# A graph layer on one core: register loads a group ahead, feed-forward weights in quarters, rounded rows in two buffers and earlier in their engine's order, a last mean in six matmuls, and multiplies in the router's wait

## The chip, the core and the metric

The program runs on one core of a Trainium2 chip. The metric is the time of one execution on the device, in microseconds (us), as the median of several runs.

## What is computed

`x` has 6250 rows of 256 values. The reference, cut to what matters (`_layernorm`, `mix` and `ffn` stand for longer functions, told in words below):

```python
xn = _layernorm(x)
m  = xn[src] @ weights[:d] + edge_attr_256 @ weights[d:]      # 106250 edges, dst sorted
h  = segment_sum(m * norm[dst][:, None], dst, 6250)           # norm = rsqrt(degree)
x  = x + (h + h_bias) + mix(xn)                               # linear attention, 8 heads, GELU block
y  = _layernorm(x)
logits = mean(y) @ Wr + br      # one router decision for all rows: two of eight experts
x  = x + layernorm(y + sum_e w_e * (gelu(y @ W1[e] + b1[e]) @ W2[e] + b2[e]))
```

The router needs the mean over all rows, so no feed-forward work on weights can start before the last row of the first part is there. All of it is float32.

## The kernel before

**Engines and semaphores.** Each engine (PE = TensorE, DVE = VectorE, ACT = ScalarE, POOL = GpSimd, SP = SyncE) has a program of its own, written by hand in the order in which it runs. It takes its instructions in that order, and `wait_ge(semaphore, value)` holds back everything behind it on that engine.

**Edge phase.** The 106250 edges are cut in 70 groups (`NG`) of three steps (`TS`), with the loop variables `t` and `q = 3 * t + i`. A step fills one of six slots of `ring`: the edges' own rows by SP (`edge_load`), and four gathers of the source rows by POOL (L562). Both wait for `s_seg` of the step that used the slot before. PE sums each strip of 128 edges into 32 destinations (`strip_sums`, L926), and turns the sums of a group over (`transposes`, L935 and L938). DVE adds them to `acc` (`sums`, L1367 and L1372): for each of four strips it first loads a place in `acc` from SBUF into a register (`value_load`, L1367), then adds there (L1372). Every two to three groups 250 rows are complete (`DONE`). PE then turns their degrees (`turn_degrees`, L948, which waits for `s_acc`, the count of DVE's additions) and multiplies by the weights (`project`, L957). The attention and mix steps are spread between these steps on all engines.

**Router.** After the last group come `last_rows`, the last rows' part of the mean (`mean_last`, L1072, eight one-column multiplies), the router's chain of small operations on one partition (DVE L1593 to L1633 and three exponentials on ACT, L872 to L877), and the loads of the chosen experts' weights by SP. ACT first normalizes the last 250 rows (`norm_last`, L734) and then loads its table of exponentials. PE turns these rows (`turn_last`, L1062), waits for the router's weights, spreads them (L1205), and starts on the feed-forward part when both halves of the first weights are split.

**Feed-forward phase.** It runs over 25 chunks `c` of 250 rows, through `chunks`: `step(0)`, `step(1)`, a loop over `step(2)` to `step(21)`, and `step(22)` to `step(24)`. All float32 operands are split into a rounded value (`_hi`, an ACT copy) and a rest (`_lo`, a DVE subtraction), and each product is three multiplies. Per chunk:

- SP loads the turned rows into `xtl`, two buffers (`fetch_turned`, L502), and stores the result (`store`, L527);
- ACT copies `xtl` to `xf_hi` (`rows_hi`), DVE makes `xf_lo` (`rows_lo`, L1638);
- PE multiplies by the first weights (`first`, L1179, 48 multiplies in four banks `q`), ACT applies the GELU (L847) and rounds to `h_hi`, DVE makes `h_lo` (L1643): both are called `hidden`;
- PE multiplies by the second weights (`second`, L1190, 48 multiplies);
- DVE adds the rows and takes mean and variance (`added`, L1651 on), POOL makes scale and offset (L618, L620), ACT applies them (`normed`, L857), DVE applies gamma and beta (`finish`, L1668 and L1671), and `store` sends the rows out.

On PE `step(c)` is `first(c + 1)`, `second(c)`. On ACT it is `rows(c + 2)`, `hidden(c + 1)`, `rows_hi(c + 2)`, `normed(c - 1)`. On DVE it is `hidden(c + 1)`, `rows_lo(c + 2)`, `finish(c - 1)`, `added(c)`. SP runs this loop, the same before and after the change but for the last chunk's store:

```python
fetch_turned(2)
for c in range(NC):
    if c + 3 < NC:
        fetch_turned(c + 3)
    store(c)                 # waits for finish(c)
```

So the load of chunk `c + 4` is issued only when the store of chunk `c` has been.

Of the kernel before, what the change touches and what calls it, by code (L numbers as in the profile page):

```python
# [83 lines left out]
def gps_layer(nc, x, src_l, dst_l, edges, wgnn, hbias, wkv_l, wq_t, bkv_l, bq_l, kln_g, kln_b, vln_g, vln_b,  # L84
              w1, b1_l, w2, b2, wr, br, fw1, fb1_l, fw2, fb2, gamma, beta, out):
    ctx = ExitStack()
    with ctx:
# [120 lines left out]
        xf_hi = sbx("xf_hi", [P, KC, CW], F32R)  # L208
        xf_lo = sbx("xf_lo", [P, KC, CW], F32R)
# [41 lines left out]
        s_w2, s_rw, s_fb = s_wkv, s_src, s_par  # L251
        W2, ROUTER, FFN_ROWS = 16 * 2 + 16, 16 + 32, 16 * 11 + 16 * 6
# [153 lines left out]
        def _(sp):  # L406
# [114 lines left out]
            sp.dma_start(grow[:, :], gamma.partition_broadcast(TN)).then_inc(s_fb, 16)  # L521
            sp.dma_start(berow[:, :], beta.partition_broadcast(TN)).then_inc(s_fb, 16)
# [11 lines left out]
            sp.wait_ge(s_out[0], 16 * (NC - NC // 2))  # L534
# [4 lines left out]
        def _(pool):  # L539
# [62 lines left out]
            pool.wait_ge(s_fb, FFN_ROWS)  # L602
# [7 lines left out]
            def step(c, u, i):  # L610
                if not (isinstance(c, int) and c + 1 >= NC):
# [3 lines left out]
                                   ALU.add).then_inc(s_xb[u], 1)  # L615
                pool.wait_ge(s_vx, c * 2 + 2)
# [10 lines left out]
        def _(act):  # L627
# [197 lines left out]
            norm_last()  # L825
# [55 lines left out]
            rows_hi(0, 0, 0)  # L881
            act.wait_ge(s_ra, 3)
# [8 lines left out]
            act.wait_ge(s_fb, FFN_ROWS)  # L891
# [860 lines left out]
```

## Time and profile before

| | |
|---|---|
| median of 3 runs | 1591.93 us (1590.64 to 1594.72) |
| profiled execution, its own time | 1609.85 us |
| its span, first to last instruction | 1608.1 us |
| PE busy | 1082.5 us, 67% of the span |
| POOL, DVE, ACT busy | 919.3, 685.6 and 530.8 us |
| mean granted TensorE clock | 0.85 |
| edge phase, about | 100 to 1287 us |
| feed-forward phase, about | 1309 to 1608 us |

The durations below come from the profiled execution, which took 17.9 us more than the median run. A busy share is an average over phases; the stages are read from windows of the trace. "Idle before, released by" names the instruction whose semaphore ended a wait, "remote" one that the trace couldn't name, and "issue" time in which the engine's own sequencer was at work or at something that the profile doesn't show: register loads stand there.

### The profile page before, as it was taken

What the parts mean: (1) busy time and instruction counts of PE and PEld (TensorE: products, weight loads), DVE (VectorE), ACT (ScalarE), POOL (GpSimd) and SP (SyncE); (2) the same over time, 40 slices, a digit from 0 to 9 for tenths busy, and PEclk for the clock granted to TensorE, in tenths of its full rate; (3) what the DMA queues carried; (4) which work ended last, traced back from release to release, by engine and by line L of the source; (5) the groups of instructions that cost most, each with busy time, mean ns of one, the idle gap of its engine ahead of it and who ended that gap; (6) DMA issues with size and microseconds to landing.
All of it is one profiled execution on the core that took longest, in us unless ns stands there. A gap on an engine that the chain in (4) does not pass through costs nothing.

```text
span 1608.1 us, 20064 instructions
## 1 busy us (share of the span) xinstructions
PE 1082.5 (67%) x6075; PEld 687.8 (43%) x6075; DVE 685.6 (43%) x1732; ACT 530.8 (33%) x1116; POOL 919.3 (57%) x974
## 2 busy tenths in 40 slices
PE   0155767666566666755776666666577759999997
PEld 0012323323223322323432333333343459999997
DVE  4733434334333344322233233242322446677675
ACT  3611111111111111111213333243233257767673
POOL 6166666676666666666666666666666103434342
PEclk9977888888877888877889778787888869999999
DMA  9975555565555555476777768777767230111111
GB/s 252 303 222 177 176 174 167 180 196 183 182 172 179 179 182 183 131 242 203 215 226 221 223 214 244 229 216 229 245 211 219 85 99 27 51 44 45 49 40 40
DMA packets 189376, 275.67 MB, mean 171 GB/s; under 512 B 19840, under 2 KB 160296, under 8 KB 188037
## 3 DMA queue, kind: packets, MB, share of 16 engines
q1 hardware_dynamic: 139424, 152.85, 31.7%
q0 software_dynamic: 39888, 108.97, 22.5%
q10 hardware_dynamic: 9975, 12.80, 2.3%
q8 instruction: 38, 0.62, 0.2%
q14 instruction: 51, 0.42, 0.1%
HBM read 248.95 MB, written 25.60 MB: 171 GB/s over the span
## 4 chain that ended last, share of the span: by engine, by line
PE 33%; another core or an unknown queue 23%; issue 18%; DVE 13%; ACT 6%; DVEq 5%; DMA 2%; SPq 1%; ACTq 0%; POOL 0%; POOLq 0%
PE bank L1190 8%; PE bank L1179 4%; PE ps_t L1179 4%; DVEq L1367 4%; PE bank L926 4%; PE bank L957 4%; PE bank L1009 3%; DVE acc L1372 2%; PE bank L1040 2%; DVE lnst L1403 1%; PE bank L1052 1%; PE ps_t L938 1%; DVE xc L1399 1%; DVE st L1227 1%
## 5 line engine op out<-in xcount | busy, mean ns | idle before, releaser
L562 POOL DMA_INDIRECT ring<-xn_table,src_sb x807 | 785.0, 973 | 441.0 <-issue 224.9
L926 PE MATMUL bank<-ring,s 128*32 128x512 f32 x1662 | 272.2, 667 | 79.6 <-DVE s L1332 38.7
L1009 PE MATMUL bank<-wstage,xt 128*125 128x512 f32 x200 | 124.2, 748 | 108.3 <-ACT xt L629 73.1
L1372 DVE TENSOR_TENSOR acc<-acc,ps_t 128x160 f32 x277 | 89.2, 322 | 203.1 <-issue 155.2
L629 ACT ACTIVATE xt<-bank 128x250 f32<-128x250 f32 (+1 forms) x75 | 33.5, 447 | 307.7 <-remote 262.4
L1040 PE MATMUL bank<-xt,p_sb 128*128 128x250 f32 x200 | 73.6, 533 | 85.6 <-ACT xt L629 44.3
L957 PE MATMUL bank<-wg,acc 128*125 128x256 f32 x400 | 123.7, 471 | 7.6 <-issue 7.6
L926 PEld LDWEIGHTS bank<-ring,s 128*32 128x32 f32 x1662 | 42.3, 115 | 197.4 <-issue 147.4
L1643 DVE TENSOR_TENSOR h_lo<-h,h_hi 128x512 fp32r<-128x512 f32 x100 | 95.8, 967 | 49.0 <-ACT h_hi L629 49.0
L618 POOL TENSOR_TENSOR rx<-vex,half 125x2 f32<-125x2 f32 x25 | 17.5, 701 | 171.8 <-DVE nmx L1664 171.8
L1190 PE MATMUL bank<-fw_hi,h_hi 128*125 128x256 f32 x400 | 111.7, 279 | 0.0
L1190 PE MATMUL bank<-fw_hi,h_lo 128*125 128x256 f32 x400 | 111.7, 279 | 0.0
L1190 PE MATMUL bank<-fw_lo,h_hi 128*125 128x256 f32 x400 | 111.6, 279 | 0.0
L1341 DVE TENSOR_TENSOR pair<-s 128x128 f32<-128x128 f32 x70 | 20.4, 291 | 202.5 <-remote 178.2
L1009 PEld LDWEIGHTS bank<-wstage,xt 128*125 128x125 f32 x200 | 41.0, 228 | 150.1 <-ACT xt L629 78.1
L957 PEld LDWEIGHTS bank<-wg,acc 128*125 128x125 f32 x400 | 92.6, 238 | 28.1 <-issue 10.2
L1040 PEld LDWEIGHTS bank<-xt,p_sb 128*128 128x128 f32 x200 | 52.6, 276 | 101.9 <-ACT xt L629 48.2
L1399 DVE TENSOR_TENSOR xc<-bank,bkv 125x512 f32<-125x512 f32 x50 | 34.4, 687 | 119.6 <-remote 105.9
L629 ACT ACTIVATE fl<-bank 128x512 f32<-128x512 f32 x70 | 41.4, 592 | 128.5 <-remote 108.3
L703 ACT ACTIVATE kvn<-xc 125x512 f32<-125x512 f32 x50 | 31.4, 628 | 153.2 <-DVE xc L1399 99.7
L1190 PEld LDWEIGHTS bank<-fw_hi,h_hi 128*125 128x125 f32 x400 | 74.3, 186 | 0.0
L1190 PEld LDWEIGHTS bank<-fw_lo,h_hi 128*125 128x125 f32 x400 | 74.2, 185 | 0.0
(224 smaller groups left out, 2147.5 us busy)
## 6 DMA issues: line engine op xcount, KB each, us to landing
ring<-edges SPq DMA_DIRECT2D x207, 512.0 KB
ring<-xn_table,src_sb POOLq DMA_INDIRECT x807
xnr<-xn_table SPq DMA_DIRECT2D x25, 250.0 KB
xch<-x SPq DMA_DIRECT2D x25, 250.0 KB
base_rows<-xch ACTq DMA_DIRECT2D x25, 250.0 KB
xt_cols<-xte ACTq DMA_DIRECT2D x25, 250.0 KB
xtl<-xt_cols SPq DMA_DIRECT2D x25, 250.0 KB, 4.9
out<-res SPq DMA_DIRECT2D x25, 250.0 KB
```

Of the source, the lines that this page charges most:

```text
L562: pool.indirect_dma_start(out=to, out_offset=None, in_=rows, in_offset=bass.IndirectOffsetOnAxis(ap=index, axis=0),).then_inc(done, 16)
L629: return nc.scalar.activation(o, i, ACT.Copy)
L926: mm = pe.matmul(ps_seg[t % 2][j * W:(j + 1) * W, :], lhsT=s32[:, t % 3, j * TS + i, :], rhs=ring[:, u, j, :], start=i == 0, stop=i == TS ...
L957: mm = pe.matmul(to, lhsT=acc[:, o, a:a + TN], rhs=wg[:, o, :], start=o == 0, stop=o == 2 * KC - 1)
L1009: mm = pe.matmul(ps_kv[0:TN, :], lhsT=xt[:, n % 2, c, 0:TN], rhs=wstage[:, c, :], start=c == 0, stop=c == KC - 1)
L1040: mm = pe.matmul(ps_kv[:, f * CW:f * CW + CN], lhsT=p_sb[:, o, f * P:(f + 1) * P], rhs=xt[:, (NT + c) % 2, o, :], start=o == 0, stop=o == ...
L1179: mm = pe.matmul(bank[q][:, (f % 2) * CW:(f % 2 + 1) * CW], lhsT=a, rhs=b, start=n == 0, stop=n == len(ops) - 1)
L1190: mm = pe.matmul(ps_o[u][0:TN, j * D:(j + 1) * D], lhsT=a, rhs=b, start=n == 0, stop=n == len(ops) - 1)
L1367: bases = [v.value_load(brow[0:1, t * ST + j:t * ST + j + 1], min_val=0, max_val=RN) for j in strips(t)]
L1372: v.tensor_tensor(acc[:, :, ds(b, W)], acc[:, :, ds(b, W)], planes[:, :, j * W:(j + 1) * W], ALU.add).then_inc(s_acc, 1)
L1399: v.tensor_tensor(xc[:, :], ps_kv[0:TN, :], bkv[:, :], ALU.add).then_inc(s_xc, 1)
L1643: v.tensor_tensor(h_lo[:, u, 2 * q:2 * q + 2, :], h32[:, 2 * q:2 * q + 2, :], h_hi[:, u, 2 * q:2 * q + 2, :].bitcast(F32), ALU.subtract).t ...
```

## The change

1. `sums` gets its registers from `strip_bases`, which is called for the next group right after this group's additions.
2. `xf_hi` and `xf_lo` get two buffers. `rows_hi(c + 2)` and `rows_lo(c + 2)` now stand ahead of `hidden(c + 1)` in ACT's and DVE's step.
3. The first weights are rounded and split in quarters; `first(0)` waits for a quarter at a time, and PE's waits for the second weights and for `b2w` stand ahead of `second(0)` and `second(1)`.
4. Gamma and beta have a semaphore of their own (`s_gb`); ACT's first `hidden` waits for the biases alone.
5. The last part of the mean is four one-column and two two-column multiplies. `norm_last` and `keep_last` move into the gaps between the exponentials.
6. PE runs 18 extra multiplies (`spin`) before it waits for the router's weights and 14 after; nothing reads their results.
7. The last chunk's second product, sums, scaling and store run in two halves.

```diff
@@ sync
             def store(c):
                 rows = out[c * CN:(c + 1) * CN, :].rearrange("(t p) d -> p t d", p=TN)
-                sp.wait_ge(s_res[c % 2], c // 2 + 1)
-                sp.dma_start(rows, res[:, c % 2, :, :]).then_inc(s_out[c % 2], 16)
+                if c < LAST:
+                    sp.wait_ge(s_res[c % 2], c // 2 + 1)
+                    sp.dma_start(rows, res[:, c % 2, :, :]).then_inc(s_out[c % 2], 16)
+                else:
+                    for j in range(2):
+                        sp.wait_ge(s_res[c % 2], c // 2 + 1 + j)
+                        sp.dma_start(rows[:, j, :], res[:, c % 2, j, :]).then_inc(s_out[c % 2], 16)
@@ scalar
-            norm_last()
             nc.scalar.activation(rt[0:1, 15, 0:1], ones[0:1, 0:1], ACT.Exp)
...
             def rows_hi(c, u, i):
                 act.wait_ge(s_tl[u], i * 16 + 16)
-                wait_past(act, s_g1, c * (FC // 2))
-                copy(xf_hi[:, :, 0:CN], xtl[:, u, :, :]).then_inc(s_xfh, 1)
+                wait_past(act, s_g1, (c - 1) * (FC // 2))
+                copy(xf_hi[:, u, :, 0:CN], xtl[:, u, :, :]).then_inc(s_xfh, 1)
...
                 if not (fixed and c + 2 >= NC):
                     rows(c + 2, u, i + 1)
+                if not (fixed and c + 2 >= NC):
+                    rows_hi(c + 2, u, i + 1)
                 if not (fixed and c + 1 >= NC):
                     hidden(c + 1, 1 - u, i + u)
-                if not (fixed and c + 2 >= NC):
-                    rows_hi(c + 2, u, i + 1)
...
             nc.scalar.activation(rt[0:1, 2, :], rt[0:1, 1, :], ACT.Exp, bias=rs[0:1, 1:2]).then_inc(s_ra, 1)
-            keep_last()
+            norm_last()
             act.wait_ge(s_rd, 16)
             nc.scalar.activation(rt[0:1, 9, :], rt[0:1, 8, :], ACT.Exp, bias=rs[0:1, 5:6]).then_inc(s_ra, 1)
+            keep_last()
...
             for j in range(2):
                 act.wait_ge(s_fw1[j], FW)
-                copy(fw1_hi[:, :, j * F:(j + 1) * F], fw1_st[:, j, :, :]).then_inc(s_w1h, 1)
+                for a in range(0, F, F // 2):
+                    copy(fw1_hi[:, :, j * F + a:j * F + a + F // 2], fw1_st[:, j, :, a:a + F // 2]).then_inc(s_w1h, 1)
...
-            act.wait_ge(s_fb, FFN_ROWS)
+            act.wait_ge(s_fb, BIASES)
@@ tensor
-                for h in range(KC):
-                    ops = [op for t in range(2 * LAST, NT) for op in ((x2[:, t, h * P:(h + 1) * P], r2[:, t:t + 1]), (ones[0:TN, :], nmr2[:, t:t + 1]))]
-                    for n, (a, b) in enumerate(ops):
-                        mm = pe.matmul(ps_f[:, h:h + 1], lhsT=a, rhs=b, start=n == 0, stop=n == len(ops) - 1)
+                for t in range(2 * LAST, NT):
+                    for h in range(KC):
+                        pe.matmul(ps_f[:, h:h + 1], lhsT=x2[:, t, h * P:(h + 1) * P], rhs=r2[:, t:t + 1], start=t == 2 * LAST, stop=False,
+                                  skip_group_check=True)
+                for t in range(2 * LAST, NT):
+                    mm = pe.matmul(ps_f[:, 0:KC], lhsT=ones[0:TN, :], rhs=nmr2[:, t:t + 1].broadcast_to([TN, KC]), start=False, stop=t == NT - 1,
+                                   skip_group_check=True)
...
-                    if f % 2 == 0 and not (isinstance(c, int) and c == 0):
+                    if f % 2 == 0 and isinstance(c, int) and c == 0:
+                        pe.wait_ge(s_w1l, 2 + q + 1)
+                    elif f % 2 == 0:
                         pe.wait_ge(s_gel, c * FC + (2 * q + 2 - FC))
...
+            def spin(n):
+
+                for t in range(n):
+                    pe.matmul(bank[0][0:TN, 0:D], lhsT=ident[0:TN, 0:TN], rhs=x2[:, t, :], start=True, stop=True)
+
+            spin(18)
             pe.wait_ge(s_top, 2)
             pe.matmul(ps_y[:, 0:2], lhsT=ones[0:1, :], rhs=rt[0:1, 13, 0:2], start=True, stop=True).then_inc(s_bp, 1)
-            pe.wait_ge(s_w1l, 4)
+            spin(14)
             first(0, 0, 0)
@@ vector
-            def sums(t):
-
-                bases = [v.value_load(brow[0:1, t * ST + j:t * ST + j + 1], min_val=0, max_val=RN) for j in strips(t)]
+            def strip_bases(t):
+
+                return [v.value_load(brow[0:1, t * ST + j:t * ST + j + 1], min_val=0, max_val=RN) for j in strips(t)]
+
+            def sums(t, bases):
+
                 v.wait_ge(s_tp, t + 1)
...
                 if i == 2 and 1 <= t <= NG:
-                    sums(t - 1)
+                    sums(t - 1, bases)
+                    bases = strip_bases(t) if t < NG else None
...
+            def added_last(j):
+
+                u, i = LAST % 2, LAST // 2
...
+                v.wait_ge(s_g2[u], i + 1 + j)
+                v.tensor_tensor(o_sb[:, u, j, :], ([ps_kv, ps_acc][u], bank[0])[j][0:TN, 0:D], xlb[:, u, j, :], ALU.add).then_inc(s_od[u], 1)
...
+            def finish_last():
...
             def step(c, u, i):
                 fixed = isinstance(c, int)
+                if not (fixed and c + 2 >= NC):
+                    rows_lo(c + 2, u, i + 1)
                 if not (fixed and c + 1 >= NC):
                     hidden(c + 1, 1 - u, i + u)
-                if not (fixed and c + 2 >= NC):
-                    rows_lo(c + 2, u, i + 1)
+                if fixed and c == LAST:
+                    added_last(0)
                 if not (fixed and c == 0):
                     finish(c - 1, 1 - u, i + (u - 1))
-                added(c, u, i)
...
+                if fixed and c == LAST:
+                    added_last(1)
+                else:
+                    added(c, u, i)
```

ACT's instructions of `step(22)`, the last that rounds a chunk's turned rows, before the change (`h32` is written by the GELUs, `h_hi` by `hidden`'s copies, `res` by `normed`):

```order
L833 ACTIVATE xl<-x2,nmr2,r2 125x256 x2
L847 ACTIVATE h32<-bank0,fb1c 128x256 x2
L629 ACTIVATE h_hi<-h32 128x512
L847 ACTIVATE h32<-bank1,fb1c 128x256 x2
L629 ACTIVATE h_hi<-h32 128x512
L847 ACTIVATE h32<-ps_t,fb1c 128x256 x2
L629 ACTIVATE h_hi<-h32 128x512
L847 ACTIVATE h32<-ps_t,fb1c 128x256 x2
L629 ACTIVATE h_hi<-h32 128x512
L629 ACTIVATE xf_hi<-xtl 128x2x250
L857 ACTIVATE res<-o_sb,bnx,rx 125x256 x2
```

And of the same step with the change:

```order
L845 ACTIVATE xl<-x2,nmr2,r2 125x256 x2
L642 ACTIVATE xf_hi<-xtl 128x2x250
L859 ACTIVATE h32<-bank0,fb1c 128x256 x2
L642 ACTIVATE h_hi<-h32 128x512
L859 ACTIVATE h32<-bank1,fb1c 128x256 x2
L642 ACTIVATE h_hi<-h32 128x512
```

In these rows the copy of the turned rows (`xf_hi`) has moved from behind four GELU pairs to ahead of them; `normed` (`res`) stays last. The loop's steps 2 to 21 have the same order.

PE between the last part of the mean and the first product, before:

```order
L1072 MATMUL bank4<-r2,x2 128x1
L1072 MATMUL bank4<-nmr2,ones 128x1
L1200 MATMUL ps_t<-wr_sb,mean_c 1x8 x2
L1062 MATMUL bank5<-ident,xle 128x125 x4
L1205 MATMUL ps_t<-rt,ones 128x2
```

And with the change:

```order
L1086 MATMUL bank4<-r2,x2 128x1 x4
L1089 MATMUL bank4<-nmr2,ones 128x2 x2
L1227 MATMUL ps_t<-wr_sb,mean_c 1x8 x2
L1077 MATMUL bank5<-ident,xle 128x125 x4
L1234 MATMUL bank0<-x2,ident 125x256 x18
L1238 MATMUL ps_t<-rt,ones 128x2
L1234 MATMUL bank0<-x2,ident 125x256 x14
L1199 MATMUL bank0<-xf_hi,fw1_hi 128x256
```

The spreading of the router's weights (L1205, now L1238) stands behind 18 new multiplies, and the first product behind 14 more.

## Rows read from the trace of the kernel before

**Rows 1.** Windows: us, busy PE, PEld, DVE, ACT, POOL, granted clock, DMA share, GB/s.

```profile
120.00:1270.00 1150.00, 748.95 (x3464) 377.10 (x3464) 405.65 (x1068) 267.64 (x572) 752.75 (x774) 0.82 0.65 199
1290.40:1314.30 23.90, 10.94 (x52) 10.37 (x53) 10.21 (x36) 13.46 (x23) 0.00 (x0) 0.50 0.47 156
1321.10:1324.50 3.40, 3.40 (x19) 3.40 (x18) 0.11 (x1) 2.44 (x5) 3.23 (x3) 0.50 0.26 73
1333.45:1580.73 247.28, 247.28 (x2114) 247.28 (x2114) 173.05 (x308) 176.64 (x372) 95.61 (x88) 1.00 0.16 44
```

**Rows 2.** Waits in 120 to 1270 us: total us, times, longest.

```profile
DVE acc L1372 <- issue: 148.8, 60, 5.3
POOL ring L562 <- remote: 144.5, 61, 4.0
PE ps_t L948 <- DVE acc L1372: 48.3, 14, 8.2
DVE acc L1372 <- ACT acc L629: 18.9, 8, 2.5
```

**Rows 3.** Timeline of DVE at one group: start, us, idle before in brackets.

```profile
637.15 0.69 DVE L1399 TENSOR_TENSOR xc<-bank,bkv 125x512 f32<-125x512 f32 x1 [2.00 <-remote]
639.84 1.69 DVE L1372 TENSOR_TENSOR acc<-acc,ps_t 128x160 f32 x4 [2.00 <-issue]
```

**Rows 4.** Timeline of all engines at the edge phase's end.

```profile
1271.09 0.30 PE L935 MATMUL ps_t<-counts,ones_r 128*128 128x128 f32 x1 [1.91 <-DVE acc L1372]
...
1275.54 1.69 DVE L1372 TENSOR_TENSOR acc<-acc,ps_t 128x160 f32 x4 [2.53 <-issue]
...
1277.37 0.37 PE L935 MATMUL ps_t<-counts,ones_r 128*128 128x32 f32 x1 [3.08 <-DVE acc L1372]
```

**Rows 5.** Timeline of all engines: a hot product, and the router's start.

```profile
1283.71 3.72 PE L957 MATMUL bank<-wg,acc 128*125 128x256 f32 x16
...
1290.85 0.56 PE L1072 MATMUL bank<-r,x 125*128 125x1 f32 x2 [2.99 <-issue]
...
1294.60 1.28 ACT L826 ACT_TABLE_LOAD   x1
...
1296.00 0.28 ACT L872 ACTIVATE rt<-rt,rs 1x8 f32<-1x8 f32 x1
```

**Rows 6.** Timeline of all engines at the start of the feed-forward phase.

```profile
1301.00 0.58 PE L1205 MATMUL ps_t<-rt,ones 1*128 1x2 f32 x2 [5.02 <-DVEq L1633]
...
1308.76 0.58 PE L1179 MATMUL bank<-xf_hi,fw_hi 128*128 128x256 f32 x1 [7.17 <-DVE fw_lo L1690]
...
1320.43 0.36 PE L1179 MATMUL bank<-xf_hi,fw_hi 128*128 128x256 f32 x1 [2.23 <-DVE b2w L1706]
```

**Rows 7.** The chain that ended last, at one feed-forward step.

```profile
1333.45 2.83 PE bank L1179 x24
...
1339.10 5.59 PE bank L1190 x48
```

**Rows 8.** Timeline of ACT over one feed-forward step.

```profile
1340.55 0.61 ACT L629 ACTIVATE xf_hi<-xtl 128x500 fp32r<-128x500 f32 x1
1341.06 1.08 ACT L857 ACTIVATE res<-o_sb,bnx,rx 125x256 f32<-125x256 f32 x2
...
1346.23 0.84 ACT L847 ACTIVATE h<-bank,fb1c 128x256 f32<-128x256 f32 x2 [3.10 <-PE bank L1179]
...
1351.85 0.61 ACT L629 ACTIVATE xf_hi<-xtl 128x500 fp32r<-128x500 f32 x1
```

**Rows 9.** Timeline of SP in the same step.

```profile
1343.62 0.31 SPq L527 DMA_DIRECT2D out<-res  x1
1344.02 0.38 SPq L502 DMA_DIRECT2D xtl<-xt_cols  x1
```

**Rows 10.** What is known of the tile `xtl`: the split of its rows, and its loads.

```profile
L1638 DVE TENSOR_TENSOR xf_lo<-xtl,xf_hi x25: 672/673/680, 1302.8 to 1577.3; 128x500 fp32r<-128x500 f32 x25
...
DMA to landing us min/median/max: 2.5/4.9/6.7
```

More of the change, by code:

```diff
@@ L615, in step @@
                                    ALU.add).then_inc(s_xb[u], 1)
+                if isinstance(c, int) and c == LAST:
+                    for j in range(2):
+                        pool.wait_ge(s_vx, LAST * 2 + 2 * j + 2)
+                        pool.wait_ge(s_bnx, LAST + j)
+                        pool.tensor_tensor(rx[:, u, j:j + 1], vex[:, u, j:j + 1], half[:, 0:1], ALU.pow).then_inc(s_rx, 1)
+                        pool.wait_ge(s_rx, LAST + j + 1)
+                        pool.tensor_tensor(bnx[:, u, j:j + 1], nmx[:, u, j:j + 1], rx[:, u, j:j + 1], ALU.mult).then_inc(s_bnx, 1)
+                    return
                 pool.wait_ge(s_vx, c * 2 + 2)
@@ L1174, in first @@
                     q = f // 2
[L1175 removed]
+                    if f % 2 == 0 and isinstance(c, int) and c == 0:
+                        pe.wait_ge(s_w1l, 2 + q + 1)
+                    elif f % 2 == 0:
                         pe.wait_ge(s_gel, c * FC + (2 * q + 2 - FC))
[L1177 removed]
+                    ops = [(a[:, k, f * P:(f + 1) * P], b[:, u, k, :]) for k in range(KC) for a, b in products((fw1_hi, xf_hi), (fw1_lo, xf_lo))]
                     for n, (a, b) in enumerate(ops):
@@ L1186, in second @@
                 wait_past(pe, s_od[u], i)
+                last = isinstance(c, int) and c == LAST
                 for j in range(2):
+                    to = bank[0][0:TN, 0:D] if last and j else ps_o[u][0:TN, j * D:(j + 1) * D]
                     ops = [(a[:, u, f, j * TN:(j + 1) * TN], b[:, f, :]) for f in range(FC) for a, b in products((h_hi, fw2_hi), (h_lo, fw2_lo))]
                     for n, (a, b) in enumerate(ops):
-                        mm = pe.matmul(ps_o[u][0:TN, j * D:(j + 1) * D], lhsT=a, rhs=b, start=n == 0, stop=n == len(ops) - 1)
-                mm.then_inc(s_g2[u], 1)
+                        mm = pe.matmul(to, lhsT=a, rhs=b, start=n == 0, stop=n == len(ops) - 1)
+                    if last or j:
+                        mm.then_inc(s_g2[u], 1)
             def step(c, u, i):
@@ L1196, in step @@
                     first(c + 1, 1 - u, i + u)
+                if fixed and c == 0:
+                    pe.wait_ge(s_w2l, 2)
+                if fixed and c == 1:
+                    pe.wait_ge(s_b2w, 1)
                 second(c, u, i)
@@ L1637, in rows_lo @@
                 v.wait_ge(s_xfh, c + 1)
-                v.tensor_tensor(xf_lo[:, :, 0:CN], xtl[:, u, :, :], xf_hi[:, :, 0:CN].bitcast(F32), ALU.subtract).then_inc(s_xfl, 1)
+                v.tensor_tensor(xf_lo[:, u, :, 0:CN], xtl[:, u, :, :], xf_hi[:, u, :, 0:CN].bitcast(F32), ALU.subtract).then_inc(s_xfl, 1)
             def hidden(c, u, i):
@@ L1664, in added @@
                 v.tensor_scalar(nmx[:, u, :], mvx[:, :, 0], -1.0, None, ALU.mult).then_inc(s_vx, 1)
+            def added_last(j):
+                u, i = LAST % 2, LAST // 2
+                if j == 0:
+                    v.wait_ge(s_xlb[u], i + 1)
+                    v.wait_ge(s_rn[u], i * 2)
+                v.wait_ge(s_g2[u], i + 1 + j)
+                v.tensor_tensor(o_sb[:, u, j, :], ([ps_kv, ps_acc][u], bank[0])[j][0:TN, 0:D], xlb[:, u, j, :], ALU.add).then_inc(s_od[u], 1)
+                v.wait_ge(s_od[u], i + 1 + j)
+                v.sem_inc(s_carry, 1)
+                v.bn_stats(st6x[:, j, :], o_sb[:, u, j, :]).then_inc(s_xs, 1)
+                v.wait_ge(s_xs, LAST * 4 + 2 * j + 1)
+                v.wait_ge(s_vx, LAST * 2 + 2 * j)
+                v.sem_inc(s_carry, 1)
+                v.bn_aggr(mvx[:, j, :], st6x[:, j, :]).then_inc(s_xs, 1)
+                v.wait_ge(s_xs, LAST * 4 + 2 * j + 2)
+                v.tensor_scalar(vex[:, u, j:j + 1], mvx[:, j, 1:2], EPS, None, ALU.add).then_inc(s_vx, 1)
+                v.tensor_scalar(nmx[:, u, j:j + 1], mvx[:, j, 0:1], -1.0, None, ALU.mult).then_inc(s_vx, 1)
+            def finish_last():
+                u, i = LAST % 2, LAST // 2
+                for j in range(2):
+                    v.wait_ge(s_rn[u], i * 2 + 1 + j)
+                    v.tensor_tensor(res[:, u, j, :], res[:, u, j, :], grow[:, :], ALU.mult).then_inc(s_rg, 1)
+                    v.wait_ge(s_rg, LAST + 1 + j)
+                    v.wait_ge(s_xb[u], i + 1)
+                    v.tensor_tensor(res[:, u, j, :], res[:, u, j, :], xb[:, u, j, :], ALU.add).then_inc(s_res[u], 1)
             def finish(c, u, i):
```

43 lines of the change are left out of this document (22 added, 21 removed).

## The prediction

> **What bounds the kernel now.** I read the windows first, since a busy share over the whole run mixes phases. In the feed-forward part PE is busy for all of the 247.28 us from `first(2)` to `first(24)`, 22 steps, at clock 1.00: PE is the bound there, at 247.28/22 = 11.24 us a step [rows 1]. The chain that ended last says the same: one half of `first` is 2.83 us for 24 multiplies, `second` 5.59 for 48, and 2.83 + 2.83 + 5.59 = 11.25 [rows 7]. In the edge part nobody is full: PE is busy 748.95 of 1150 us, POOL 752.75 [rows 1]. The waits say what holds them. DVE loses 148.8 us in 60 stops ahead of its additions, released by "issue": the four register loads, 2.5 us a group. POOL waits 144.5 us for ring slots, so POOL is not the bound; it waits for PE's strip sums. PE itself loses 48.3 us in 14 waits of `turn_degrees` for `acc` [rows 2]. The last groups show it small: 2.53 us of loads, the addition of 1.69, and PE, which waited 3.08 [rows 4]. In the router and at the start of the feed-forward part, the timeline of all engines is read for gaps [rows 5, 6]. Last I read ACT, SP and the tile `xtl` over one steady step, since the order on ACT changes and SP's loop does not [rows 8 to 10].
>
> **The change part by part.** All is summed against the profiled execution, 1609.85 us with a span of 1608.1. It stood 17.9 us above the median of 1591.93; I carry the sum over to the median unchanged.
>
> *Rounded rows ahead of `hidden`: +49.9 us.* The extra buffer costs nothing and PE's work stays. But ask what the load of a chunk hangs on. SP issues the load of chunk k behind the store of chunk k-4, in the same loop as before. That store waits for `finish(k-4)`, which waits for `normed(k-4)`, the last thing of ACT's step. Before, ACT copied the turned rows just ahead of `normed`, so the way round from landing to landing held only the copy, `normed`, the store and the load: 0.05 + 0.51 + 2.56 + 0.40 + 4.9 = 8.42 us, by the rows below, well under 11.24. Now the copy stands ahead of `hidden`, and the wait for the load holds back all four GELU pairs, then `normed`, then the store, then the next load. The step has become a loop through the DMA:
>
> - landing to the start of the copy: some 0.05, my choice, no row shows it alone;
> - copy to the next ACT instruction: 1341.06 - 1340.55 = 0.51 [rows 8];
> - `hidden`, four GELUs and roundings: 1351.85 - 1346.23 = 5.62 [rows 8];
> - start of `normed` to the issue of the store: 1343.62 - 1341.06 = 2.56 [rows 8, 9];
> - store to the issue of the load: 1344.02 - 1343.62 = 0.40 [rows 9];
> - load to landing: 4.9, the median of 25 [rows 10].
>
> That is 14.04 us a step against PE's 11.24, so 2.80 us more for each step in which the loop binds. It doesn't bind at once. Chunk 4's load is issued at 1344.02 and lands at about 1348.9 [rows 9]; with its copy and split (0.51 and 0.67 [rows 8, 10], and small gaps) the rows are ready at about 1349.8 (as early as before, since this first load has not been round the loop). PE wants them for `first(4)` at 1333.45 + 2 x 11.24 = 1355.93, so there are 6.1 us in hand. From chunk 4 to chunk 24 the loop goes round 20 times: 20 x 2.80 - 6.1 = +49.9. The loss would begin at chunk 7, when 3 x 2.80 has used up the 6.1. Bounds: the fastest landing in the trace is 2.5 and the slowest 6.7 [rows 10]. With 2.5 the loop is 11.64, and 20 x 0.40 = 8.0 is less than the 8.5 then in hand: nothing. With 6.7 it is 15.84: 20 x 4.60 - 4.3 = +88. I take the median, because the loads of the steady part stand behind a store on SP, as they will after the change.
>
> The Trainium skill, "DMA: Bandwidth & Descriptors", section "Anatomy of one DMA", fits a DMA as 2.0 us fixed plus its bytes over 436e3 per us, for a path from GpSimd; the 256,000 bytes of this load would land in about 2.6 us, an estimate. By that rule the loop would be 11.74, the term 20 x 0.50 - 8.4 = +1.6 and the whole about 1569; the row has 4.9 in place of 2.6, and the sum goes by the row.
>
> *Register loads a group ahead: -18.* The four loads still cost DVE 2.5 us a group, but behind the additions. DVE's timeline at one group shows 2.00 us of them between a wait's end and the addition of 1.69 [rows 3]. They are worth something only where PE waits for that addition: 14 waits, at most 2.5 each, so at most 35 [rows 2]. Where DVE would come to the additions early anyway, or where ACT is what `acc` waits for (8 times, 18.9 us [rows 2]), the gain is nothing, and the loads now stand ahead of DVE's next attention work. PE feels `acc` in none of the other groups. I take half of 35, -18, with -45 (PE's 48.3 nearly all gone) and +6 (the loads late for what comes next) as ends.
>
> *End of the edge part: -4.* The 2.53 ahead of the last additions goes, and of the 1.91 ahead of that group's turn 1.5 [rows 4]: -4.0.
>
> *Mean and exponentials: -1.1.* Sixteen PE records become twelve; the first pair takes 0.56 [rows 5] with its start, so four records save at most 1.1, and I take 0.85. The table load of 1.28 no longer stands behind `norm_last`, and the first exponential starts at 1296.00 [rows 5]; most of it is behind DVE, so I add 0.25.
>
> *Spins, quarters, biases: -1.5, between -3 and +8.* A multiply of this size takes 3.72/8 = 0.465 us at full clock [rows 5] and up to 0.93 at half, and the router runs at 0.50 [rows 1]. The 18 cost between 8.4 and 16.7; I take four cold and 14 hot, 10 us. They start when the last rows are turned, between 1296.00 and 1301.00 [rows 5, 6]; I take 1297.5, and so an end near 1307.5. But the router's weights were spread at 1301.00 [rows 6]: now at 1307.5, 6.5 us late. What hangs on them, DVE's splitting of the first weights, slides, but meets the 14 further spins, 6.5 us. So `first(0)` starts near 1314.5, not 1308.76, but at full clock, and waits no more for all halves. It takes 5.65 and ends at 1320.1, `first(1)` was at 1320.43 behind a wait of 2.23 for `b2w` [rows 6], which is gone, and so is the cold stretch at 0.50 behind it [rows 1]. 1320.4 + 5.65 + 5.59 = 1331.7 to 1332 against 1333.45: -1.5. If the spins take 16.7 it is +5 to +8.
>
> *Last chunk in halves: +0.5, between -2 and +2.* Overlap of the two halves saves about half of `normed` and `finish`, under 2 us; with the step late, ACT comes to the last `hidden` about as much later.
>
> Sum: +49.9 - 18 - 4 - 1.1 - 1.5 + 0.5 = **+25.8**: 1635.7 for the profiled execution, **1618** for the median.
>
> **The rivals.** *B, faster: the loop doesn't bind.* Its place is the load's landing. The point from which it decides is a period of 11.24 + 6.1/20, about 11.5 us, for no loss at all, and of about 12.75 (a landing of 3.6) for a change of zero, since the other terms give 24. The loads at the start landed in 2.5 to 2.8, with no store ahead; for it speaks also that a loop that waits has more idle DMA. Against it: the DMA share in the steady part is 0.16 [rows 1], so there is little load to be rid of, and 4.9 is the median of all 25. With nothing for the loop, 1591.93 - 18 - 4 - 1.1 - 1.5 + 0.5 = 1567.8.
>
> *C, about the same: the register loads are worth all of PE's waits.* 48.3 in place of 18 gives 1617.7 - 30.3 = 1587.4, just under no change. For it: POOL has 144.5 us of waits to give, so a PE that goes ahead is not held by gathers at once. Against it: a wait of 8.2 can't be cut by loads of 2.5.
>
> *D, slower yet: each wait costs clock.* After the 2.23 us wait at 1320.43, PE ran at 0.50 from 1321.1 to 1324.5 [rows 1, 6]. With 2.8 us of waiting in each step such a stretch may come back in each. One of 3.4 us costs 1.7 of work, and 11.24 + 1.7 = 12.9 is still under the loop's 14.04: no cost. If all of `first` ran at half, a step would be 2 x 5.66 + 5.59 = 16.9, PE would bind again, and some 17 steps of 2.9 more would give 1618 + 49 = 1667.
>
> The Trainium skill, "TensorE: Matmul & The Clock Gate", section "HAM oscillation — how this bites in real kernels", says that a wait before each tile can make each tile start throttled; here one such wait was followed by 0.50, and the steady steps have none to test it on.
>
> **How the numbers follow.** I give the forecast 0.73, B 0.14, C (and landings of about 3.6) 0.07, D 0.06. The range takes in the forecast's own bounds: landing 5.5 and nothing for the register loads is 20 x 3.40 - 5.5 = 62.5 in place of 49.9 and 0 in place of -18, 1648; landing 4.0, 20 x 1.90 - 7.0 = 31, with -25 for the loads gives 1592. With C it reaches to 1586; B and D stay out. So 1586 to 1648. This measurement can tell about 0.3% (4.8 us) from no change. Faster: B and half of C, 0.17; same: 0.05; slower: 0.78.
>
> **What the profile after would show.** Right: ACT waits ahead of `xf_hi` in steps 2 to 22, released by the load of `xtl`; loads are issued 14.0 us apart; PE idles 2.8 us ahead of each `first` from chunk 7 on and is busy 80% of the window; GELUs no longer wait for PE. In the edge part no issue time ahead of `acc`, and PE's 48.3 fallen to about 30. The spins end after 1307, later than their weights. Wrong: loads 11.24 us apart with PE gapless (B); PE's `turn_degrees` no longer waiting at all (C); a granted clock below 0.8 in the steady steps with PE without idle time (D). The size is most open in the landing time: each 0.1 us of it moves the result by 2.1.

## The result, and the profile after

The median went from 1593.33 to 1636.19 us; the ratio is 1.0264 (95% interval 1.0244 to 1.0285), 42 us slower by the ratio (the medians differ by 42.9; here and below the microseconds of a change go by the ratio). 1618 was forecast, in a range of 1586 to 1648. The profiled execution took 1635.94 us, its span 1634.1.

Windows of the changed kernel over 15 steady steps (columns as in [rows 1]):

```profile
1380.00:1590.00 210.00, 180.23 (x1440) 177.18 (x1440) 100.69 (x210) 120.28 (x255) 51.05 (x60) 0.96 0.13 37
```

PE is busy 180.23 of 210 us where it was busy for all of the window before, and the granted clock is 0.96 where it was 1.00. PE has become an engine that waits. The timeline of ACT, start, us, and idle before in brackets, over one step:

```profile
1393.34 0.62 ACT L642 ACTIVATE xf_hi<-xtl 128x500 fp32r<-128x500 f32 x1 [5.85 <-DMA xtl<-xt_cols]
1393.87 0.82 ACT L859 ACTIVATE h<-bank,fb1c 128x256 f32<-128x256 f32 x2
...
1399.43 1.08 ACT L870 ACTIVATE res<-o_sb,bnx,rx 125x256 f32<-125x256 f32 x2
...
1407.36 0.62 ACT L642 ACTIVATE xf_hi<-xtl 128x500 fp32r<-128x500 f32 x1 [5.86 <-DMA xtl<-xt_cols]
```

The copies are 14.02 us apart; before they stood 11.30 apart [rows 8]. From landing to landing the rows give 0.11 to the start of the copy, 0.53 to the first GELU, 5.56 for `hidden`, 2.56 from `normed` to the store, 0.39 to the load and 4.86 to its landing: 14.01 in sum. ACT, which waited 3.10 us for PE in a step, now waits 5.85 for the load, with the GELUs and `normed` behind that wait. SP's timeline holds the other half of the way round:

```profile
1387.98 0.29 SPq L528 DMA_DIRECT2D out<-res  x1
1388.37 0.38 SPq L502 DMA_DIRECT2D xtl<-xt_cols  x1
1401.99 0.29 SPq L528 DMA_DIRECT2D out<-res  x1
1402.38 0.38 SPq L502 DMA_DIRECT2D xtl<-xt_cols  x1
```

And the chain that ended last goes through these: the load, GELU pairs (here with 1.72 us of PE between two of them), `normed`, the two operations of `finish`, the store, the next load.

```profile
1388.37 4.86 DMA xtl<-xt_cols
...
1393.87 0.83 ACT h L859 x2
...
1400.54 0.70 DVE res L1733
1401.27 0.70 DVE res L1736
1401.99 0.29 SPq L528
...
1402.38 4.86 DMA xtl<-xt_cols
```

On PE's timeline there is a wait ahead of each `first` from chunk 7 on, 18 in all, released by a GELU that frees a bank. It is 2.4 to 2.5 us in twelve steps and 0.9 to 1.0 in six:

```profile
1380.90 0.39 PE L1199 MATMUL bank<-xf_hi,fw_hi 128*128 128x256 f32 x1 [2.52 <-ACT h L859]
...
1394.92 0.38 PE L1199 MATMUL bank<-xf_hi,fw_hi 128*128 128x256 f32 x1 [2.51 <-ACT h L859]
...
1408.93 0.38 PE L1199 MATMUL bank<-xf_hi,fw_hi 128*128 128x256 f32 x1 [0.97 <-ACT h L859]
```

The start of the feed-forward part, on the timeline of all engines:

```profile
1274.19 9.31 PE L1234 MATMUL bank<-x,ident 125*125 125x256 f32 x36
...
1283.43 0.38 PE L1238 MATMUL ps_t<-rt,ones 1*128 1x2 f32 x2
...
1283.74 6.31 PE L1234 MATMUL bank<-x,ident 125*125 125x256 f32 x28
...
1289.69 0.47 PE L1199 MATMUL bank<-xf_hi,fw_hi 128*128 128x256 f32 x1
```

The 18 extra multiplies take 9.3 us and end right where the router's weights are spread: those waited for the spins, no longer for DVE's chain [rows 6].

Waits of the edge part, 120 to 1270 us:

```profile
POOL ring L567 <- remote: 132.3, 61, 3.8
DVE s L1363 <- issue: 124.8, 51, 4.7
...
PE ps_t L963 <- DVE acc L1406: 18.2, 6, 11.0
...
PE ps_t L963 <- DVE acc L1414: 8.0, 3, 4.8
```

The 148.8 us of register loads ahead of `acc` [rows 2] are gone; 124.8 stand ahead of `s`, the next group's one-hot rows.

**A table by stage.** All stages are read from the timelines, in us: from the end of the last strip sum to the end of the last four-strip addition and the one behind it (`acc`); on to the means' product with the router's weights; on to `first(0)`; on to `second(0)`; on to the end of `first(24)`; on to the end of the span. All kernels of this study are in it, the experiments described below. The column "strips end" is where that last strip sum ended.

| kernel | strips end | acc | means | first(0) | second(0) | first(24) | end |
|---|---|---|---|---|---|---|---|
| before | 1269.2 | 9.9 | 15.6 | 14.0 | 18.9 | 258.7 | 21.7 |
| changed | 1252.6 | 5.0 | 13.7 | 18.5 | 12.7 | 308.5 | 23.3 |
| a1, order back | 1267.4 | 4.9 | 13.4 | 19.2 | 12.8 | 258.7 | 19.6 |
| a2, load ahead of store | 1269.0 | 4.9 | 13.6 | 19.1 | 12.7 | 258.7 | 19.5 |
| b1, before, copy first | 1268.5 | 10.3 | 16.1 | 13.6 | 18.9 | 310.0 | 23.9 |
| b2, before, registers ahead | 1265.4 | 6.9 | 14.5 | 14.1 | 19.9 | 258.7 | 21.7 |
| a3, order back, registers at use | 1109.6 | 8.0 | 14.4 | 19.2 | 12.7 | 258.7 | 19.5 |
| a4, order back, no spins | 1116.0 | 4.9 | 11.8 | 12.8 | 14.4 | 260.2 | 19.5 |
| a5, load at store | 1114.8 | 5.0 | 12.2 | 18.7 | 12.8 | 258.7 | 20.4 |
| b3, before, fixed places | 1108.5 | 4.5 | 14.0 | 13.6 | 19.0 | 258.7 | 21.7 |
| c0, as a1 | 1118.5 | 5.0 | 12.0 | 19.0 | 12.7 | 258.7 | 19.5 |
| c1, short spins | 1114.0 | 5.0 | 13.5 | 11.8 | 12.8 | 264.9 | 19.5 |
| c2, normed ahead | 1118.3 | 5.0 | 13.0 | 18.8 | 12.7 | 258.7 | 19.6 |
| c3, as a4 | 1116.1 | 5.1 | 13.5 | 11.8 | 14.4 | 260.5 | 19.6 |

The first column differs by up to 160 us between executions of nearly the same edge part. Where the code is the same, `acc` and `means` still differ by up to 1.9 us between executions, the next two columns by up to 1.0, and the last two by at most 0.3. So ratios are taken only within one chip, and from the spans the later stages alone are compared; each row is one execution.

### The profile page after: what moved, and what is told of

Read it like the earlier page. It is cut to its first block, busy times and chain, and to the rows that moved or that the text cites. A ratio compares the mean times of both kernels' runs of the same rounds, so it can differ in the third digit from the quotient of the medians.

```text
span 1634.1 us, 20218 instructions
## 1 busy us (share of the span) xinstructions
PE 1109.5 (68%) x6135; PEld 694.9 (43%) x6135; DVE 666.2 (41%) x1739; ACT 530.5 (32%) x1118; POOL 904.0 (55%) x976
## 3 DMA queue, kind: packets, MB, share of 16 engines
q1 hardware_dynamic: 139429, 152.85, 31.2%
## 4 chain that ended last, share of the span: by engine, by line
another core or an unknown queue 12%; PE 11%; issue 9%; DVE 7%; ACT 7%; DMA 5%; DVEq 2%; ACTq 1%; SPq 0%; POOL 0%; POOLq 0%
DMA xtl<-xt_cols 5%; PE bank L1199 4%; ACT h L859 3%; DVEq L1398 2%; PE bank L1212 2%; DVE acc L1406 1%; ACT res L870 1%; PE ps_t L1199 1%; PE bank L1067 1%; PE bank L1234 1%; DVE res L1733 1%; DVE res L1736 1%; PE bank L941 1%; DVE xch L1455 1%
## 5 line engine op out<-in xcount | busy, mean ns | idle before, releaser
L941 PE MATMUL bank<-ring,s 128*32 128x512 f32 x1662 | 282.2, 671 | 81.7 <-DVE s L1363 56.7
L1024 PE MATMUL bank<-wstage,xt 128*125 128x512 f32 x200 | 131.6, 791 | 109.8 <-ACT xt L642 69.0
L972 PE MATMUL bank<-wg,acc 128*125 128x256 f32 x400 | 108.6, 419 | 18.3 <-issue 17.8
L1055 PE MATMUL bank<-xt,p_sb 128*128 128x250 f32 x200 | 68.5, 503 | 60.2 <-ACT xt L642 56.1
L1372 DVE TENSOR_TENSOR pair<-s 128x128 f32<-128x128 f32 x70 | 20.4, 291 | 201.2 <-remote 167.8
L1363 DVE TENSOR_TENSOR s<-iota,rel 128x384 f32<-128x384 f32 x70 | 38.8, 554 | 146.9 <-issue 132.8
L1679 DVE TENSOR_TENSOR h_lo<-h,h_hi 128x512 fp32r<-128x512 f32 x100 | 71.6, 717 | 66.1 <-ACT h_hi L642 66.1
L972 PEld LDWEIGHTS bank<-wg,acc 128*125 128x125 f32 x400 | 79.0, 204 | 36.0 <-issue 24.3
L1199 PE MATMUL bank<-xf_hi,fw_hi 128*128 128x256 f32 x200 | 62.1, 310 | 35.9 <-ACT h L859 35.9
L1055 PEld LDWEIGHTS bank<-xt,p_sb 128*128 128x128 f32 x200 | 49.3, 259 | 78.2 <-ACT xt L642 63.7
```

The source lines that it names most:

```text
L941: mm = pe.matmul(ps_seg[t % 2][j * W:(j + 1) * W, :], lhsT=s32[:, t % 3, j * TS + i, :], rhs=ring[:, u, j, :], start=i == 0, stop=i == TS ...
L972: mm = pe.matmul(to, lhsT=acc[:, o, a:a + TN], rhs=wg[:, o, :], start=o == 0, stop=o == 2 * KC - 1)
L1024: mm = pe.matmul(ps_kv[0:TN, :], lhsT=xt[:, n % 2, c, 0:TN], rhs=wstage[:, c, :], start=c == 0, stop=c == KC - 1)
L1055: mm = pe.matmul(ps_kv[:, f * CW:f * CW + CN], lhsT=p_sb[:, o, f * P:(f + 1) * P], rhs=xt[:, (NT + c) % 2, o, :], start=o == 0, stop=o == ...
L1199: mm = pe.matmul(bank[q][:, (f % 2) * CW:(f % 2 + 1) * CW], lhsT=a, rhs=b, start=n == 0, stop=n == len(ops) - 1)
L1363: v.tensor_tensor(s32[:, t % 3, 0:m, :], iota[:, 0:W].unsqueeze(1).broadcast_to([P, m, W]), wide(rel[:, c:c + m], m, W), ALU.is_equal).the ...
```

## The experiments

### Round one: which part costs, and by which mechanism

The kernel before took 1605.89 us on this chip.

**a1: the order put back.** On ACT, and the same with `rows_lo` on DVE:

```diff
-                if not (fixed and c + 2 >= NC):
-                    rows_hi(c + 2, u, i + 1)
                 if not (fixed and c + 1 >= NC):
                     hidden(c + 1, 1 - u, i + u)
+                if not (fixed and c + 2 >= NC):
+                    rows_hi(c + 2, u, i + 1)
```

> The changed kernel with the copy and the split of the turned rows put back behind the four GELU pairs, on ACT and DVE; the two buffers and all else stay. Theory 1 (the step is a loop through load, GELUs, store and next load, 14.02 us long in the trace after, against 11.24 of PE's work): the way round from landing to landing falls to about 8.4 us, PE has no gaps from first(2) on, loads are issued 11.24 us apart, and the time falls by about 50 us to 1586. Rival (the place on ACT is harmless; the extra buffer, another address or the load itself is what slows): loads stay 14.0 us apart and the time stays at 1636.

Measured: 1595.15 us, 0.9933 of before (0.9919 to 0.9946). Its windows have PE full again:

```profile
1340.00:1560.00 220.00, 220.00 (x1882) 220.00 (x1881) 154.31 (x273) 157.64 (x332) 84.11 (x77) 1.00 0.16 45
```

Without the reorder the change is a gain of 0.7%, with it a loss of 2.6%.

**a2: each load a store earlier.**

```diff
             fetch_turned(2)
+            fetch_turned(3)
             for c in range(NC):
-                if c + 3 < NC:
-                    fetch_turned(c + 3)
+                if c + 4 < NC:
+                    fetch_turned(c + 4)
                 store(c)
```

> The changed kernel with SP's loads issued a step earlier: fetch_turned(c + 4) stands ahead of store(c), and waits only for the split of chunk c + 2. Theory 1: the loop is cut, since the next load no longer hangs on the store; the copy ahead of the GELUs is then harmless, and the time is that of the order put back, about 1586, within 3 us. Rival (the copy ahead of the GELUs is what costs, by delaying hidden or by the clock): it stays above 1620.

Measured: 1597.06 us, 0.9937 (0.9923 to 0.9950). The copy stands ahead of the GELUs here, and nothing is lost: the load of chunk `c + 4` hangs on the store of chunk `c - 1` in place of `c`, so one way round now carries two loads. It is not the place on ACT that costs, but that place together with a load that must wait for the newest store.

**b1: only the copy first.** Before, with item 2's two buffers and order.

```diff
-        xf_hi = sbx("xf_hi", [P, KC, CW], F32R)
+        xf_hi = sbx("xf_hi", [P, 2, KC, CW], F32R)
...
+                if not (fixed and c + 2 >= NC):
+                    rows_hi(c + 2, u, i + 1)
                 if not (fixed and c + 1 >= NC):
                     hidden(c + 1, 1 - u, i + u)
```

> The kernel before with only the two buffers and the copy and split ahead of hidden. Theory 1: a step of 14.0 us, PE idle 2.8 us in each from about the seventh, and 1593 + 50 = 1643. If the loss in the changed kernel needs another part of the change (the quarters, the spins), this one stays near 1593.

Measured: 1658.49 us, 1.0325 (1.0310 to 1.0340), 52 us more. No other part of the change is needed for the loss.

**b2: only the registers ahead.** Before, with item 1 (`strip_bases`, called right behind `sums`).

```diff
-                    sums(t - 1)
+                    sums(t - 1, bases)
+                    bases = strip_bases(t) if t < NG else None
```

> The kernel before with only the register loads a group ahead. Theory 1, as predicted: 18 us less, 1575. The rival that the medians suggest (the median rose by 43 where the profiled spans differ by 26, so the profiled execution of before was long in its edge part and the loads are hidden in most executions): within 5 us of 1593, while the issue idle time ahead of acc is gone from the trace all the same.

Measured: 1600.95 us, 0.9961 (0.9948 to 0.9975), 6.3 us less (4.9 by the medians), not 18. The waits of 120 to 1270 us:

```profile
DVE s L1332 <- issue: 134.1, 52, 4.6
POOL ring L562 <- remote: 129.5, 58, 3.3
...
PE ps_t L948 <- DVE acc L1375: 33.2, 8, 11.8
...
PE ps_t L948 <- DVE acc L1383: 8.7, 2, 6.6
...
PE ps_t L948 <- DVE acc L1381: 7.1, 1, 7.1
```

PE's waits for `acc` sum to 33.2 + 8.7 + 7.1 = 49.0 us against 48.3 in [rows 2], though no load stands ahead of an addition any more. But one execution's sum says little: b1, with the edge part of the kernel before, has 35.5, a1 37.8, and the changed kernel 26.2.

### Round two: the landing, the registers' bound, the spins

Another chip: the kernel before took 1449.12 us.

**a5: the load just ahead of the store, at the same moment.**

```diff
             fetch_turned(2)
+            fetch_turned(3)
             for c in range(NC):
-                if c + 3 < NC:
-                    fetch_turned(c + 3)
+                if c + 4 < NC:
+                    sp.wait_ge(s_res[c % 2], c // 2 + 1)
+                    fetch_turned(c + 4)
                 store(c)
```

> The changed kernel with each load still held until the result of chunk c is finished, but issued just ahead of the store instead of behind it. It measures whether a landing of 4.9 us comes from the store ahead of it on the queue. If it does, the load lands in about 2.6 as at the start, the way round is 14.02 - 0.40 - 2.3 = 11.3 us, and the time is near that of the order put back (0.995 of before). If the load takes 4.9 us in any case, the way round is 13.6 us and the time is 20 x 2.4 - 6.5 = 41 us above it (1.02 of before).

Measured: 1444.42 us, 0.9965 (0.9947 to 0.9982). What is known of `xtl`, and SP's timeline:

```profile
DMA to landing us min/median/max: 2.6/2.8/7.8
```

```profile
1225.02 0.32 SPq L502 DMA_DIRECT2D xtl<-xt_cols  x1
1225.39 0.33 SPq L528 DMA_DIRECT2D out<-res  x1
1236.62 0.32 SPq L502 DMA_DIRECT2D xtl<-xt_cols  x1
1236.99 0.33 SPq L528 DMA_DIRECT2D out<-res  x1
```

The loop is still there, but two instructions changing places took it from 14.02 to about 11.5 us, and that much, 0.3 over PE's step for 20 steps, is covered by what is in hand. The landing of 4.9 us came from the store ahead of it.

**b3: no register loads at all.** Before, with the places of this input as constants in a table, `PLACES`.

```diff
-                bases = [v.value_load(brow[0:1, t * ST + j:t * ST + j + 1], min_val=0, max_val=RN) for j in strips(t)]
+                bases = [PLACES[t * ST + j] for j in strips(t)]
```

> The kernel before with the places of the additions written in as constants of this input, so that there are no register loads at all (it leaves out the loads; the sums are the same for this input). It bounds what moving the loads can ever bring. Theory 1 now (the loads were mostly hidden, since something else, the round of ring slots through gathers, strip sums and the clock, sets the edge part): no more than the 5 to 6 us of the loads a group ahead, 0.995 to 0.997 of before. Rival (the loads only moved onto DVE's next work, and DVE holds PE up there as well): 15 to 40 us faster, 0.975 to 0.99.

Measured: 1442.88 us, 0.9952 (0.9931 to 0.9974): 7 us, between 4 and 10, for taking the loads away altogether, on this chip.

**a3: order back, registers at their use again.** Item 1 undone on a1.

> The changed kernel with the turned rows' order put back and the register loads at their use again. With the loads ahead the kernel with the order back stood at 0.9933 of before, and the loads alone at 0.9961. If the loads' gain adds to the rest, this one stands at about 0.997 of before (5 us of gain from the start of the feed-forward part and the tail, the loads' 5 to 6 us gone). If the gain of the loads comes only together with the rest, it stands at 0.993 or at 1.000.

Measured: 1445.23 us, 0.9977 (0.9965 to 0.9989), near the 0.997 of parts that add up; the two ratios behind that 0.997 are of the first chip. On this chip the groups of the edge part (busy, mean ns | idle before and what ended it, 120 to 1100 us) are, in a3,

```profile
L567 POOL DMA_INDIRECT ring<-xn_table,src_sb x766 | 746.9, 975 | 233.4 <-issue 227.3 <-PE bank L941 6.1
L941 PE MATMUL bank<-ring,s 128*32 128x512 f32 x1528 | 246.6, 721 | 253.9 <-DMA ring<-xn_table,src_sb 246.2 <-DVE s L1363 4.0 <-DMA ring<-edges 3.5
```

and on the first chip, in a1,

```profile
L567 POOL DMA_INDIRECT ring<-xn_table,src_sb x671 | 655.0, 976 | 326.5 <-issue 188.0 <-remote 112.2 <-PE bank L941 26.4
L941 PE MATMUL bank<-ring,s 128*32 128x512 f32 x1344 | 215.7, 665 | 20.8 <-DMA ring<-edges 10.6 <-issue 9.4
```

In a3 POOL has next to no slack: it is busy for 746.9 of the 980 us, its own issue takes 227.3, and 6.1 are left for waits; PE waits 246.2 us for gathers. So DVE's loads have little to hold up there before the end; that is argued from these rows, and b3's 7 us fit it.

**a4: order back, no spins.** Both `spin` calls taken out of a1.

> The changed kernel with the order put back and without both runs of extra multiplies. By my sum the spins delay the spreading of the router's weights by 6.5 us and give a full clock to the first products in return, so without them first(0) starts earlier and runs partly at a granted clock of 0.5: within 2 us of the kernel with the order back (0.9933 of before). If the spins are pure delay, it is 4 to 6 us faster (0.990); if the clock is worth more than the delay, 3 us slower or more (0.995).

Measured: 1439.38 us, 0.9935 (0.9914 to 0.9957). By the table `first(0)` comes 6.4 us earlier than in a3, and 1.7 and 1.5 us are given back behind it. Its 0.9935 can't be held against a1's 0.9933, which is of another chip; c3 and c0 make that comparison.

### Round three: on one chip beside each other

The kernel before took 1450.19 us.

**c0: a1 once more.**

> The changed kernel with the turned rows' order put back, once more, to stand on one chip beside the next three. 0.993 of before as at first; if the chips differ in the edge part only, the microseconds gained are the same, 7 to 11.

Measured: 1445.20 us, 0.9962 (0.9948 to 0.9976), 5.5 us; on the first chip it was 10.8. That the microseconds would be the same was wrong: less is gained on this chip. That POOL has no slack in the edge part here would explain it, but isn't shown to be the cause.

**c3: a4 once more.**

> The order put back without extra multiplies, beside the same with them on one chip. The traces give first(0) 6.3 us earlier after the means' product, 1.6 us more for the first chunk and 1.5 us more for the second, both at a lower granted clock: 3 us faster than the order put back with spins. If the spins pay, it is slower.

Measured: 1443.14 us, 0.9956 (0.9943 to 0.9969). The intervals of c0 and c3 overlap: by the timed runs the spins are worth nothing that can be told, either way. By the stages from the means' product to the end, 306.3 against 309.9 in c0, they cost 3.6 us; a4 against a3 gives 3.2. Of what comes back behind a later `first(0)`, only the first part is clock, where c3's expectation put both down to it: the 1.8 us behind `second(0)` hold a wait of 1.61 at a granted clock of 1.00, for chunk 2's copy.

**c1: short spins.** 5 and 12 in place of 18 and 14, on a1.

> The order put back, with 5 and 12 extra multiplies in place of 18 and 14. The router's weights come about 6.5 us after the means' product, and the last rows are turned after 4: 5 multiplies fit between, 18 run 6 us past. Theory: the weights are spread about 5 us earlier than with 18, first(0) starts 4 to 6 us earlier than with 18, and most of it at full clock, so 3 to 5 us faster than the order put back. Rival: with only 5 the clock isn't granted in time, the 12 and part of first(0) run at 0.50, and the gain over no spins is nothing.

Measured: 1443.20 us, 0.9952 (0.9939 to 0.9966), 2 us under c0 by the medians, with overlapping intervals, and not the 3 to 5 expected. `first(0)` starts 7.2 us earlier than in c0 and at a granted clock of 1.00, and 6.2 of it are lost again between `second(0)` and `first(24)`: 3.31 in the only wait there, and most of the rest by the 5.7 us behind it at a granted clock of 0.50. PE's timeline and that window:

```profile
1166.05 0.55 PE L1199 MATMUL bank<-xf_hi,fw_hi 128*128 128x256 f32 x1 [3.31 <-ACT xf_hi L642]
```

```profile
1166.10:1171.80 5.70, 5.70 (x27) 5.70 (x28) 2.98 (x8) 1.75 (x5) 3.40 (x4) 0.50 0.00 0
```

That is chunk 2's copy, which in a1's order stands behind the GELUs of chunk 1. With a start this early the copy ahead of the GELUs may pay. No run shows it (a2 or c2 with short spins); by the table it could give back at most 264.9 - 258.7 = 6.2 us.

**c2: `normed` ahead too.** The changed kernel, its copy ahead of the GELUs, and

```diff
+                if not (fixed and c == 0):
+                    normed(c - 1, 1 - u, i + (u - 1))
                 if not (fixed and c + 1 >= NC):
                     hidden(c + 1, 1 - u, i + u)
-                if not (fixed and c == 0):
-                    normed(c - 1, 1 - u, i + (u - 1))
```

on ACT, with `finish` moved likewise on DVE.

> The changed kernel with the copy still ahead of hidden, but normed and finish of the chunk before also moved ahead of hidden, on ACT and DVE. Theory 1: what made the loop long was hidden standing between a load's landing and the store that releases the next load; with normed ahead of it the way round is about 10 us or less, PE runs without gaps, and the time is within 3 us of the order put back. Rival (a copy ahead of hidden costs in itself, or waiting for the sums ahead of hidden makes hidden late): loads 12 to 14 us apart and 20 us or more slower.

Measured: 1442.88 us, 0.9950 (0.9936 to 0.9964), with the loads still behind the stores. This takes the GELUs out of the way round, where a2 made each load wait for one store less and a5 took out the store's part of it; all three end the loss.

## Why the prediction was right, and where not

**The loop, +49.9: right in mechanism and size.** From `second(0)` to the end of `first(24)` the changed kernel takes 308.5 us against 258.7: +49.8. The period was put at 14.04 and is 14.02; the landing at 4.9, and it is 4.86. PE's first gap is ahead of `first(7)`, as worked out: `second(5)` begins at 1358.6 and `first(7)` at 1366.9, 8.3 later where 5.6 was the rule. b1 shows that the reorder alone does it, a1 that nothing is left without it, and a2, a5 and c2 that it is a loop, since easing it at three different places ends the loss. Only what PE shows was told wrongly in part. Its wait is released by a GELU that frees the bank, a moment after the split. Where the wait is 2.5 us, `first` starts 2.79 us after the last multiply of `second`, which fits the 2.8; in the six steps with less than 1.0, PE had worked for 3.4 us at a granted clock of 0.50 before. PE is busy 86% and not 80% for this reason, and because the last multiply's record runs for 0.28 us where the next would start after 0.12.

**Register loads, -18: wrong in size, -6.3 by b2.** The failed step is "half of 35": each of PE's waits for `acc` was taken to shrink by up to the loads' 2.5 us, and the kernel's time with them. In b2 the waits didn't shrink in sum (49.0 against 48.3), though the changed kernel has 26.2, near the 30 forecast: a sum that stands at 48.3 and at 35.5 in two executions of the same edge part (before and b1) is no measure of the time. b3 gives 7 us for no loads at all on the second chip, so there all of DVE's time in loads was worth no more. The stage table says where: 3.0 us in b2 and 5.4 in b3 (3.5 against a3, of b3's chip) lie between the last strip sum and the last addition, when nothing overlaps any more. What sets the rest is, by a3's rows, POOL where it is full; on the first chip, where POOL waits for slots and PE hardly for gathers, no run settles it.

**End of the edge part, -4: right**, 9.9 to 5.0 us; but it is most of what the loads bring, not an addition to it. The two terms together were -22 and measured -6.3. The profiled spans differ by 26.0, which looks as though -22 had come true. By b2 it hadn't: the one execution profiled before was 17.9 us above its median and the one after 0.3 us below. This difference of executions stood in for the gain. It was carried over to the median unchanged, and there it had nothing to stand on.

**Mean and exponentials, -1.1**: the stage to the means' product went from 15.6 to 13.7; but it is 14.0 in b3 and 14.5 in b2, where its code is that of before, so no more than this is known.

**Spins, quarters, biases, -1.5: right in sum.** From the means' product to `second(0)`: 32.9 to 31.2. The spins put `first(0)` off by 4.5 us (5.7 was worked out), and 6.2 come back behind it. The first 18 took 9.3 us, where 10 was taken. c1 and c3 show that most of what comes back is owed to the other parts (quarters, semaphores, PE's waits): without spins `second(0)` is at 26.2, and with short ones at 24.6.

**Tail, +0.5: +1.6.** The halves save 2.1 us (21.7 to 19.6 in a1), and the late `hidden(24)` costs 3.7 more.

**The rivals.** B, a landing of 2.5, would have been right on the loop had the load stood ahead of the store: a5 is that case, and its loop binds nothing. C is refuted by b2 (6.3 in place of 48.3) and, on the second chip, by b3 (7). D came in its harmless half, and only in six of the 18 steps: a stretch of 3.4 us at 0.50 costs 1.5 to 1.7 us, and the wait ahead of the next `first` is that much shorter. The windows of a step at full clock, of such a stretch, and of the step around it, each step window beginning in the last 0.9 us of a wait, are

```profile
1380.00:1394.00 14.00, 11.51 (x96) 11.31 (x96) 6.71 (x15) 8.02 (x18) 3.38 (x4) 1.00 0.14 37
1396.40:1399.80 3.40, 3.40 (x18) 3.40 (x17) 1.63 (x3) 3.34 (x8) 0.00 (x0) 0.50 0.00 0
1394.00:1400.50 6.50, 5.58 (x34) 5.58 (x35) 3.44 (x5) 6.37 (x15) 0.00 (x0) 0.74 0.00 0
1400.50:1408.00 7.50, 7.46 (x64) 7.25 (x63) 3.27 (x9) 1.64 (x5) 3.44 (x4) 1.00 0.25 68
```

so the clock falls behind some of the waits, returns within the step, and the loop's own slack pays for it. The Trainium skill, "TensorE: Matmul & The Clock Gate", section "HAM oscillation — how this bites in real kernels", tells of a kernel in which every tile starts throttled behind its wait. Here 12 of the 18 waits had no such start behind them, and the measurement decides; it cost nothing, because PE wasn't the bound any more.

Sum of what was measured: +49.8 + 1.6 for the loop and tail, 48.5 to 44.9 = -3.6 for the stages between the last addition and `second(0)`, and -6.3 by b2: +41.5 against a measured 42. The -3.6 is the difference of two single executions, good to 1 or 2 us. Of the 16 us by which the forecast of +25.8 fell short, 15.7 are the -22 of the edge part that measured -6.3. The range held, since its upper end had counted nothing for the register loads.

## What to carry to other kernels

Before an instruction is moved ahead on an engine, follow what it waits for back to its issuer, and ask whether that issuer waits for something that now stands behind the instruction. If so, the two make a loop, and its period is a sum that the rows of one step give beforehand: here 14.04 against 14.02. In this kernel a way out of two or three lines was at the queue: a load that needs nothing of the store is put ahead of it.

Where one engine's idle time is long but others are full or wait for each other, taking work off it may be worth little more than it is at the ends, where nothing overlaps: here 6.3 us out of 148.8. And a sum made against one profiled execution is compared with medians term by term, since two executions can differ by more than a term.

## What the runs showed of the hardware

A load of 250 KB issued 0.4 us behind a store of the same size on SP's queue landed in 4.9 us (the median in every kernel here but a5), and issued 0.37 us ahead of it in 2.8 (a5). The Trainium skill, "DMA: Bandwidth & Descriptors", section "Anatomy of one DMA", whose fit is for a DMA issued by GpSimd, would give about 2.6, an estimate; this load is issued by SP. The 2.8 of a5 is near it, and behind a store the measurement is nearly double.

The same kernel took 1593, 1606, 1449 and 1450 us in four sets of runs. Nearly all of it lies in the edge part, which ends some 150 us earlier in the second and third round: there PE waits for gathers and POOL hardly for anything, in the first round POOL waits for ring slots and PE hardly for gathers. What makes the first one slower stays open. The 258.7 us from `second(0)` to the end of `first(24)` are the same in all rounds, wherever PE has no wait there.
